# Perceiver layer on one core: latent keys of the mix spread over all 128 partitions, two matmuls for three

## The reference

```python
xn = layernorm(x, ln_x_g, ln_x_b)            # context, 1024 rows a batch
ln = layernorm(latents, ln_l_g, ln_l_b)      # latents, 64 rows a batch
q = (ln @ Wq).reshape(b, m, h, d).transpose(0, 2, 1, 3)
kv = jnp.concatenate([xn @ Wkv, ln @ Wkv], axis=1)
...
sim = jnp.einsum('bhid,bhjd->bhij', qn, kn)
...
attn = jax.nn.softmax(sim.astype(jnp.float32), axis=-1).astype(sim.dtype)
out = jnp.einsum('bhij,bhjd->bhid', attn, v)
```

## Time and profile before

| | |
|---|---|
| median of the runs | 247.27 us |
| span of the profiled execution | 245.1 us |
| TensorE matmul busy | 232.6 us (95%) |
| VectorE busy | 154.8 us (63%) |
| ScalarE busy | 150.8 us (62%) |
| GpSimd busy | 79.6 us (32%) |
| chain that ended last | TensorE 74%, VectorE 13% |
| mean granted TensorE clock | 0.991 |

### The profile page before, as it was taken

The page is one execution under the profiler, slowest core; times in us unless marked ns, Lnnn a source line. Parts: engine busy times, 40 slices in busy tenths (PEclk is TensorE's granted clock), DMA queues, the critical chain, the costliest instruction groups (busy, mean ns, idle before and its releaser), DMA issues.

```text
span 245.1 us, 4234 instructions
## 1 busy us (share of the span) xinstructions
PE 232.6 (95%) x1509; PEld 199.7 (81%) x1509; DVE 154.8 (63%) x345; ACT 150.8 (62%) x328; POOL 79.6 (32%) x112
## 2 busy tenths in 40 slices
PE   6689999998999999999999999999999999999995
PEld 6464887876788888888888879999999888899884
DVE  1779999997687776867667655566664441303441
ACT  4354688877866768686756567777686754104141
POOL 5468776884453536464140600000000000100200
PEclk9799999999999999999999999999999999999999
DMA  5882111010000000000000899400000000000000
GB/s 180 306 276 95 47 28 38 21 45 0 21 3 0 0 4 1 0 3 0 0 3 0 261 417 322 121 3 0 0 4 0 3 1 0 3 0 0 3 0 21
DMA packets 11077, 13.67 MB, mean 56 GB/s; under 512 B 1553, under 2 KB 9777, under 8 KB 10801
## 3 DMA queue, kind: packets, MB, share of 16 engines
q1 hardware_dynamic: 10784, 12.88, 15.9%
q10 hardware_dynamic: 272, 0.52, 0.6%
HBM read 13.14 MB, written 0.13 MB: 54 GB/s over the span
## 4 chain that ended last, share of the span: by engine, by line
PE 74%; DVE 13%; DMA 3%; ACT 3%; issue 3%; POOL 2%; SPq 1%; ACTq 0%; POOLq 0%; DVEq 0%
PE banks L1103 23%; PE banks L991 13%; PE banks L1036 9%; PE banks L1065 8%; PE banks L1125 5%; PE banks L1222 4%; DVE small L761 4%; DMA rows<-in_L_xattn_ln_x_b 3%; PE banks L1118 3%; DVE sk L773 3%; PE banks L1067 3%; PE banks L1152 2%; DVE raw L729 2%; PE banks L1247 1%; DVE small L735 1%
## 5 line engine op out<-in xcount | busy, mean ns | idle before, releaser
L797 DVE TENSOR_TENSOR ptl<-banks,pth 128x512 fp32r<-128x512 f32 (+1 forms) x48 | 26.6, 555 | 32.6 <-ACT pth L562 32.0
L1103 PE MATMUL banks<-xnh,pth 128*128 128x256 f32 x128 | 37.5, 293 | 0.0
L1103 PE MATMUL banks<-xnl,pth 128*128 128x256 f32 x128 | 36.1, 282 | 0.0
L1103 PE MATMUL banks<-xnh,ptl 128*128 128x256 f32 x128 | 36.1, 282 | 0.0
L451 POOL TENSOR_TENSOR small<-small 128x16 f32<-128x16 f32 x8 | 23.3, 2907 | 35.4 <-DVE small L768 35.4
L562 ACT ACTIVATE pth<-banks 128x512 fp32r<-128x512 f32 (+1 forms) x48 | 23.6, 492 | 12.6 <-PE banks L991 10.9
L508 ACT ACTIVATE sk<-banks 128x512 f32<-128x512 f32 x36 | 20.6, 604 | 14.3 <-PE banks L1036 14.2
L413 POOL TENSOR_SCALAR tsm<-tsm 128x1 f32<-128x1 f32 x2 | 0.4, 190 | 88.8 <-DVE tsm L726 88.8
L773 DVE TENSOR_TENSOR sk<-banks,small 128x512 f32<-128x512 f32 x36 | 22.9, 678 | 7.2 <-POOL small L451 7.2
L761 DVE TENSOR_REDUCE small<-sk 128x8 f32<-128x512 f32 x36 | 23.5, 677 | 3.7 <-ACT sk L508 3.7
L1103 PEld LDWEIGHTS banks<-xnh,pth 128*128 128x128 f32 x128 | 24.4, 191 | 0.4 <-issue 0.4
(11 more groups left out here) (176 smaller groups left out, 494.1 us busy)
## 6 DMA issues: line engine op xcount, KB each, us to landing
knT<-in_L_attn_qkv_kernel SPq DMA_DIRECT2D x1, 3072.0 KB, 13.7
raw<-in_ctx SPq DMA_DIRECT2D x16, 128.0 KB, 2.0
knT<-in_L_xattn_Wq SPq DMA_DIRECT2D x1, 1024.0 KB, 9.2
wv<-in_L_xattn_Wkv SPq DMA_DIRECT2D x1, 1024.0 KB, 5.2
wout_sb<-in_L_xattn_Wout SPq DMA_DIRECT2D x1, 1024.0 KB, 5.5
knT<-in_L_attn_out_kernel SPq DMA_DIRECT2D x1, 1024.0 KB, 16.3
wraw<-in_L_xattn_Wkv ACTq DMA_DIRECT2D x1, 512.0 KB, 4.1
wraw<-in_L_xattn_Wkv SPq DMA_DIRECT2D x1, 512.0 KB, 6.4
```

What stands on the lines that cost most here:

```text
L797: nc.vector.tensor_tensor(ptl[0:rows_, j0:j1, :], banks[0:rows_, t3_bank(u, c), 0:(j1 - j0) * P].rearrange("p (j r) -> p j r", j=j1 - j0), ...
L1103: last = nc.tensor.matmul(banks[:, u_bank(u), 0:D], p_[0:r, j, :], x_, start=(j == 0 and i == 0), stop=(j == NB - 1 and i == 2))
```

## The change

The latent rows go to all 128 partitions: `lat2` holds the 64 rows of a batch twice, on partitions 0 to 63 and on 64 to 127, by four transfers. `lnhl` holds the rounded rows, and GpSimd then replaces the upper 64 partitions by what the rounding left. In `sp2` each unit gets 64 more columns. After the exponentials of a unit GpSimd copies the 64 latent columns there (`latents_twice`), so the ninth block is 128 columns, the latent probabilities twice, and its transpose fills all partitions. Two products over 128 partitions then give high by high and high by low (`pth` by `lnhl`), and low by high with low by low added (`ptl` by `lnhl`).

```diff
-        lnh = sb("lnh", [M, B, D], F32R)
-        lnl = sb("lnl", [M, B, D], F32R)
+        lnhl = sb("lnhl", [P, B, D], F32R)
...
-        sp2 = sb("sp2", [P, 2, KW])
+        sp2 = sb("sp2", [P, 2, KW + M])
...
-        lat64 = early(0, 0, B * D)[0:M, :].rearrange("p (b d) -> p b d", b=B)
+        lat2 = early(0, 0, B * D).rearrange("p (b d) -> p b d", b=B)
...
                     for b in range(B):
-                        sp.dma_start(lat64[:, b, :], lnf[b * M:(b + 1) * M, :]).then_inc(w_lat, 16)
+                        for half in range(2):
+                            sp.dma_start(lat2[half * M:(half + 1) * M, b, :], lnf[b * M:(b + 1) * M, :]).then_inc(w_lat, 16)
...
+            def latents_twice(u):
+
+                pool.wait_ge(exp_ready, u + 1)
+                nc.gpsimd.tensor_copy(sp2[:, u % 2, KW:KW + M], sp2[:, u % 2, J:KW]).then_inc(twice_ready, 1)
...
+                if i >= ITEMS_A - 1:
+                    latents_twice(i - ITEMS_A + 1)
                 if i == ITEMS_A - 1:
+
                     pool.wait_ge(lnh_ready, 1)
-                    nc.gpsimd.tensor_tensor(lnl[:, :, :], lat64, lnh[:, :, :].bitcast(F32),
+                    pool.wait_ge(twice_ready, 1)
+                    nc.gpsimd.tensor_tensor(lnhl[M:P, :, :], lat2[M:P], lnhl[M:P, :, :].bitcast(F32),
                                             ALU.subtract).then_inc(lns_ready, 1)
-
+                    pool.wait_ge(lns_ready, 1)
+
+            for u in range(ITEMS - ITEMS_A + 1, UNITS):
+                latents_twice(u)
...
-                    act.wait_ge(w_lat, 16 * B)
-                    nc.scalar.activation(lnh[:, :, :], lat64, ACT.Copy).then_inc(lnh_ready, 1)
+                    act.wait_ge(w_lat, 16 * 2 * B)
+                    nc.scalar.activation(lnhl[:, :, :], lat2, ACT.Copy).then_inc(lnh_ready, 1)
...
+                if c == 2:
+                    pe.wait_ge(twice_ready, u + 1)
...
-                        r = block_of(u, j)[1]
-                        xh = xnh[:, b * NT + j, :] if j < NT else lnh[:, b, :]
-                        xl = xnl[:, b * NT + j, :] if j < NT else lnl[:, b, :]
+                        if j == NT:
+
+
+                            nc.tensor.matmul(banks[:, u_bank(u), 0:D], pth[:, j, :], lnhl[:, b, :], start=False, stop=False)
+                            last = nc.tensor.matmul(banks[:, u_bank(u), 0:D], ptl[:, j, :], lnhl[:, b, :], start=False,
+                                                    stop=True)
+                            continue
+                        xh = xnh[:, b * NT + j, :]
+                        xl = xnl[:, b * NT + j, :]
                         for i, (p_, x_) in enumerate(((pth, xh), (pth, xl), (ptl, xh))):
-                            last = nc.tensor.matmul(banks[:, u_bank(u), 0:D], p_[0:r, j, :], x_, start=(j == 0 and i == 0),
-                                                    stop=(j == NB - 1 and i == 2))
+                            nc.tensor.matmul(banks[:, u_bank(u), 0:D], p_[:, j, :], x_, start=(j == 0 and i == 0), stop=False)
```

More of the change, by code:

```diff
@@ L222, in perceiver_layer @@
         exp_ready = sem("exp_ready")
+        twice_ready = sem("twice_ready")
         rinv_ready = sem("rinv_ready")
@@ L342, in block_of @@
         def block_of(u, j):
-            return sp2[:, u % 2, j * P:j * P + (P if j < NT else M)], (P if j < NT else M)
+            return sp2[:, u % 2, j * P:(j + 1) * P]
         T3 = [(0, 4), (4, 8), (8, NB)]
@@ L541, in exponentials @@
                 act.wait_ge(max_ready, u + 1)
-                nc.scalar.activation(sp2[:, u % 2, :], sp2[:, u % 2, :], ACT.Exp, bias=nmax[:, u:u + 1], scale=-1.0,
+                nc.scalar.activation(sp2[:, u % 2, 0:KW], sp2[:, u % 2, 0:KW], ACT.Exp, bias=nmax[:, u:u + 1], scale=-1.0,
                                      accum_out=rsum[:, u:u + 1]).then_inc(exp_ready, 1)
@@ L560, in probs_high @@
                 act.wait_ge(u_ps, u)
-                rows_ = block_of(u, j0)[1]
-                nc.scalar.activation(pth[0:rows_, j0:j1, :], banks[0:rows_, t3_bank(u, c), 0:(j1 - j0) * P].rearrange(
+                nc.scalar.activation(pth[:, j0:j1, :], banks[:, t3_bank(u, c), 0:(j1 - j0) * P].rearrange(
                     "p (j r) -> p j r", j=j1 - j0), ACT.Copy).then_inc(pth_ready, 1)
@@ L783, in logits_max @@
                     dve.wait_ge(pt_ps, 3 * (u - 1))
-                nc.vector.tensor_tensor_reduce(out=sp2[:, u % 2, :], in0=logits_ps, in1=mbias[:, u // G, :], scale=-1.0,
+                nc.vector.tensor_tensor_reduce(out=sp2[:, u % 2, 0:KW], in0=logits_ps, in1=mbias[:, u // G, :], scale=-1.0,
                                                scalar=BIG, op0=ALU.add, op1=ALU.min,
@@ L794, in probs_low @@
                 j0, j1 = T3[c]
-                rows_ = block_of(u, j0)[1]
                 dve.wait_ge(pth_ready, 3 * u + c + 1)
-                nc.vector.tensor_tensor(ptl[0:rows_, j0:j1, :], banks[0:rows_, t3_bank(u, c), 0:(j1 - j0) * P].rearrange(
-                    "p (j r) -> p j r", j=j1 - j0), pth[0:rows_, j0:j1, :].bitcast(F32), ALU.subtract).then_inc(ptl_ready, 1)
+                nc.vector.tensor_tensor(ptl[:, j0:j1, :], banks[:, t3_bank(u, c), 0:(j1 - j0) * P].rearrange(
+                    "p (j r) -> p j r", j=j1 - j0), pth[:, j0:j1, :].bitcast(F32), ALU.subtract).then_inc(ptl_ready, 1)
             def unit_low(u):
@@ L1080, in probs_transposed @@
                     pe.wait_ge(ptl_ready, 3 * u + c - (1 if u == G and c == 2 else 0))
-                transposes(banks[:, t3_bank(u, c), :], lambda i: block_of(u, j0 + i)[0], j1 - j0,
-                           width=block_of(u, j0)[1]).then_inc(pt_ps, 1)
+                transposes(banks[:, t3_bank(u, c), :], lambda i: block_of(u, j0 + i), j1 - j0).then_inc(pt_ps, 1)
             def mix(u, parts=(0, 1, 2)):
```

## The result

The changed kernel takes **276.96 us**, the median of four runs; one of them fell far out (566.81 us), the other three lie between 276.5 and 277.1, with 276.83 in the middle. The kernel before, timed beside it, takes 247.12 us (246.79 to 247.66). The ratio is 1.119 (95% interval 1.117 to 1.122): slower by 29.8 us. The forecast was 279.4 us, with a range of 266 to 288. The profiled execution has a span of 275.3 us against 245.1, so **30.2 us** more are to be found in the trace.

The account below looks back on a forecast made before the run. TensorE, busy 95% of the span, was taken to bound the kernel. Stalls of 25.2 us, less 2.9 gained, plus 9.8 for clock falls add 32.1 to 247.3, giving 279.4 us, range 266 to 288.

Parts of the forecast that it names:

- GpSimd's queue: Turns 0 to 7: copy ahead of the power delays key transposes, 2.9 us a turn, 4.9 in turn 0, together 25.2.
- The clock: TensorE's pauses in the first half: clock falls in seven of eight turns, 1.4 us each, 9.8 us.
- rival (1): First-half turns: the stalls come but TensorE's clock holds, 269.6 us; chance 0.24.
- rival (2): First-half turns: the clock stays low for a second stretch in each turn, 292.2 us; chance 0.07.
- TensorE's gain: Latent block of the mix: one product fewer and no slow starts, 0.40 us a unit, 2.9 us reaching the end.
- Rival (4): Latent block: slow starts remain and only one product a unit is saved, 281.3 us; chance 0.05.
- Small edits: Additional latent transfers, wider transposes, TensorE's wait for the copy, rounded-latent copy: zero; 1.1 us once if transfers lose cover.
- Rival (3), faster: GpSimd's moved power is not what the keys wait for, so no pause arises, 241.9 us; chance 0.04.

Follow-up runs that it names:

- the pause filled: Changed kernel with identity matmuls in TensorE's wait ahead of the key transposes, eleven a turn and nineteen in turn 0: 268.06 us, ratio 1.084.
- the copies alone: Kernel before, keeping its three half-array products, with the sixteen copies added behind the power on GpSimd: 247.51 us, ratio 1.0005.
- the first experiment: Changed kernel with each copy moved behind the power on GpSimd and the latent subtraction back ahead of the attention: 241.15 us, ratio 0.974.

## Why the prediction held

**GpSimd's queue: right.** A stall of 2.9 us a turn was forecast for turns 1 to 7; undisturbed turns show 13.87 against 11.10, 2.77. Turn 0 was forecast at 4.9 and shows 5.1 (15.47 against 10.37 with the pause filled). Together 25.2 against 25.0. The copy, a bound from two rows with 0.25 taken, measured 0.24. The chain had the links that the prediction had listed, in that order.

**The clock: right, the least certain term.** Seven falls in eight turns, as forecast, at 1.3 us each on average against 1.4: 9.4 against 9.8 us. The sizes were less even than I had them. The difference between the changed kernel and the one with its pause filled is 0.83 us in turn 0, 2.29 in turn 1, 1.06, 1.39 and 1.18 in turns 2 to 4, nothing in turn 5, 1.48 and 1.18. That rival (1), the clock holding, was wrong rests on the pause: fill it, and the clock holds. Its time of 269.6 us is close to the 268.06 measured then. Where the prediction said that a fall costs at most 1.6 to 1.7 us, it had taken the length of one low stretch from the start of the program for the length of all. In turn 1 the clock stayed low for about 6.8 us, twice as long as in the others, which is rival (2) in one turn of eight.

**TensorE's gain: right mechanism, one size off.** The step that failed in size is the gain of 0.40 us a unit, 0.12 for the product and 0.28 for slow starts around the 64-row operands. It is 0.52 in the turns 11 to 14, 0.12 and 0.40, and these carry most of the gain. I had read the starts of unit 8, where transposes follow, and taken them for all units. Where two `attended` products follow, they are slowed too (0.54 us in place of 0.43). Where transposes of probabilities follow, the gain is 0.35 and the 0.40 was a little too high: two full products take 0.24, but the transposes then start 0.41 after the last full product and not 0.36. What reaches the end was forecast at 2.9 us and came to 3.3. Turns 8 to 10 gained 0.32, 0 and 0.19 (forecast 0.37, 0.02 and 0.3), the four behind them 0.49 to 0.52 each. Rival (4), slow starts that stay, is excluded by the start distances of 0.12.

**Small edits: right, with one thing missed.** The copy and its wait cost nothing; the copies alone show it, 247.51 against the 247.38 of before timed beside it. The additional transfers and the wider transposes were not tested by themselves. Of the 0.52 us that a turn gained, the starts shown above hold 0.51, which leaves nothing for the transposes. From the centring to the first exponentials it is 7.42 us with two transfers and 7.41 with four; a cost ahead of that place, below the microsecond by which the executions wander, would not be seen. What I missed is that moving the subtraction also *removes* something, the clash with VectorE's centring, 0.86 us between the two traces. I had listed what the moved instruction delays and not what it had been delaying.

**Rival (3), faster,** was wrong for this order of the instructions, and its price was right for the other. It said that if the power did not wait for the copy, the time would be 241.9 us; the first experiment measured 241.15. In its trace the eight turns gain 1.8 us, where the rival said up to 2.5, what lies behind them 3.4 against 2.9, and the start 0.3. The start is the 0.93 us of the clash, which the rival did not have, less 0.6 by which this execution came later to that place.

Against the forecast of the span, 277.2, the measured 275.3 is 1.9 lower: 0.9 from the ports, 0.4 from the gain, 0.4 from the clock and 0.2 from the stall.

## What to carry to other kernels

An instruction's own cost (0.24 us, sixteen times) says nothing about what it costs in a list that runs in order. Ask what it waits for and what stands behind it: a wait for a late event, put ahead of an early and long piece of work, moves all of that work behind the event. Here moving the copy one place back is worth 33 us, and with the subtraction in its old place it turns a change that is 12% slower into one that is 2.5% faster than the kernel before. And when a pause arises in TensorE's work, price it together with its clock; matmuls that nobody needs, put into the pause, bring back the second part, and only that.

## What the runs showed that I had not expected

- GpSimd's subtraction of 64x512 stretches a VectorE operation of 0.40 us to 1.45 when both start together, and leaves it alone when it starts 0.2 us later. A fifth of a microsecond in the start of one instruction decides 0.93 us up to the first exponentials.
- A block on 64 of the 128 rows costs 0.40 us beyond its products where matmuls of the output projection follow, a quarter of it in these matmuls, and 0.23 where transposes of probabilities follow.
- The clock fell in turn 7 after a pause of 1.67 us that it had survived six times; in the changed kernel it did not fall in turn 5 after 2.78 us. What decides this was not settled.
- The lower clock costs in uneven portions, 0.8 to 1.5 us in six turns and 2.3 in the one where it stayed low twice as long.
